# Two-layer graph network on one Trainium2 core: first gathers of the large aggregation issued in its own block, and two table stores moved to GpSimd's queue

## The reference

```python
# layer 0: 4 heads of 256, D_IN = 1024
xp = (x @ W).reshape(N, H, C)
e = leaky_relu(a_src[src] + a_dst[dst])           # edges and self loops
alpha = softmax of e over the edges of one dst
out = segment_sum(xp[src] * alpha, dst) + bias
x = layernorm(x + relu(out))
# layer 1: 1024 -> 256 -> attention with 4 heads of 64 -> 1024
h = rmsnorm(x) @ W_down
xl, xr = h @ Wl, h @ Wr
e = att . leaky_relu(xl[src] + xr[dst])
x = layernorm(x + segment_sum(softmax(e) * xl[src], dst) @ W_up)
```

## Time and profile before

| | us |
|---|---|
| median of 3 runs | 2424.14 (2420.76 to 2429.64) |
| profiled execution: its own time | 2423.4 |
| its span, first to last instruction | 2421.6 |
| projection block, with its boundary | 123 to 636 |
| large aggregation | 636 to 1209 |
| node block | 1209 to 1447 |
| edge scores of layer 1 | 1447 to 1991 |

### The profile page before, as it was taken

The page is one execution under the profiler, slowest core; times in us unless marked ns, Lnnn a source line. Parts: engine busy times, 40 slices in busy tenths (PEclk is TensorE's granted clock), DMA queues, the critical chain, the costliest instruction groups (busy, mean ns, idle before and its releaser), DMA issues. The chain is left out here.

```text
span 2421.6 us, 50236 instructions
## 1 busy us (share of the span) xinstructions
PE 1890.9 (78%) x10689; PEld 1240.5 (51%) x10690; DVE 1622.0 (67%) x4091; ACT 845.9 (35%) x2902; POOL 1377.3 (57%) x1421
## 2 busy tenths in 40 slices
PE   3988888887488888888848866877777773799797
PEld 2543334434266665666546654555555552667543
DVE  6345455448566666666668856656666569799987
ACT  1300000001477777777746633000000002455465
POOL 1077777771477777777600008777777762566500
PEclk9989999998799999999979988999999996899999
DMA  6433333220599999999899936888888873777457
GB/s 230 120 87 71 68 76 74 65 54 18 196 363 356 360 361 356 361 361 360 324 277 275 281 130 189 246 230 251 242 234 243 230 224 106 251 250 257 162 186 225
DMA packets 255893, 529.81 MB, mean 219 GB/s; under 512 B 52188, under 2 KB 148197, under 8 KB 255769
## 3 DMA queue, kind: packets, MB, share of 16 engines
q0 software_dynamic: 92672, 258.83, 33.2%
q1 hardware_dynamic: 125251, 225.64, 28.3%
q10 hardware_dynamic: 37878, 44.27, 6.7%
HBM read 439.07 MB, written 102.49 MB: 224 GB/s over the span
## 5 line engine op out<-in xcount | busy, mean ns | idle before, releaser
L155 POOL DMA_INDIRECT acc<-xl_table,csrc x392 | 400.6, 1022 | 354.6 <-POOLq L1299 235.4
L1195 ACT ACTIVATE wone<-onehot,w 128x64 f32<-128x64 f32 x1760 | 432.2, 333 | 166.1 <-DVE onehot L1239 162.1
L155 POOL DMA_INDIRECT ga<-a_src_table,csrc x316 | 315.8, 999 | 156.7 <-issue 143.8
L1212 PE MATMUL banks<-w_sb,wone 128*64 128x256 f32 x2368 | 315.6, 392 | 93.8 <-ACT wone L1195 45.2
L930 PE MATMUL banks<-w_sb,acc 128*128 128x512 f32 x800 | 381.5, 622 | 0.0
L155 POOL DMA_INDIRECT w_sb<-xp_table,isrc x296 | 293.9, 993 | 148.3 <-DMA xp_table<-xp_st 58.4
L1235 DVE TENSOR_TENSOR acc<-banks,acc 128x512 f32 x440 | 304.3, 692 | 0.3 <-issue 0.3
L1664 PE MATMUL banks<-xr_parts,onehot_t 128*128 x1320 | 188.1, 286 | 127.9 <-issue 102.6
L1796 PE MATMUL banks<-msg,onehot 128*128 128x265 f32 x880 | 216.5, 400 | 37.2 <-POOL msg L1766 17.4
L1692 DVE SCALAR_TENSOR_TENSOR prod<-banks,att_relu 128x1024 f32<-128x1024 f32 x110 | 134.7, 1224 | 163.9 <-ACT w L1629 157.5
L1664 PEld LDWEIGHTS banks<-xr_parts,onehot_t 128*128 128x128 bf16 x1320 | 127.2, 96 | 211.5 <-issue 172.2
(11 more groups left out here) (315 smaller groups left out, 2746.2 us busy)
## 6 DMA issues: line engine op xcount, KB each, us to landing
edge_rows<-acc SPq DMA_DIRECT2D x440, 130.0 KB
rows<-edge_rows SPq DMA_DIRECT2D x55, 1040.0 KB, 4.9
lt_bc<-local_dst ACTq DMA_DIRECT2D x110, 128.0 KB, 3.0
lt<-local_dst ACTq DMA_DIRECT2D x110, 128.0 KB, 4.3
xp_table<-xp_st SPq DMA_DIRECT2D x25, 512.0 KB, 2.9
w<-acc SPq DMA_DIRECT2D x100, 128.0 KB, 3.5
xpt<-xp_table SPq DMA_DIRECT2D x25, 512.0 KB, 4.9
x_table<-y SPq DMA_DIRECT2D x25, 512.0 KB, 7.0
```

What stands on the lines that cost most here:

```text
L155: return self.pool.indirect_dma_start(out, None, table, bass.IndirectOffsetOnAxis(ap=idx, axis=0), bounds_check=self.bound, oob_is_err=False)
L1195: last = nc.scalar.activation(wone[:, s, j, h, :], onehot[:, s, j, :], ACT.Copy, scale=w9[:, bass.ds(g * U + j, 1), h:h + 1].rearrange("p ...
L1212: nc.tensor.matmul(psum[WN * a:WN * (a + 1), j, k * C:(k + 1) * C], wone[:, s, j, h, :], slots[r][:, j, h * C:(h + 1) * C], start=True, st ...
```

## The change

It has two parts. In the first, POOL no longer issues gathers in the projection block: all 440 are issued in the aggregation block, behind the clearing of slots 22 to 24, which moves there too, and behind the wait for the stores. Slots 12 to 15 are cleared by ACT, as four activations that copy with scale 0, behind `take_weights`; slots 16 to 19 by DVE, two at a time between its `first_weights`. DVE waits for the stores of `xp_st` before it clears `rows_c`, and for POOL's clearing (`s_zero`) before its first addition. In the second part the stores of `x1` and `xl` are issued by POOL, with lags 3 and 6 in place of 4 and 7. A third edit only writes a bounded register value to a register of its own.

```diff
@@ projection block, POOL
-                    gather.wait(s_xp, NT)
-                    for i in range(2):
-                        gather.wait(s_xs[i], 16 * ((NT + 1 - i) // 2))
-                    for g in range(FIRST):
-                        for j in range(U):
-                            gather.rows_of(rows[:, g, j, :], xp_t, isrc[:, g * U + j:g * U + j + 1]).then_inc(s_r[g][j], 16)
-                    nc.gpsimd.memset(acc[:, NU:NT, :], 0.0)
@@ projection block, ACT, at its end
+                    for i in range(4):
+                        nc.scalar.activation(acc[:, KEPT + i, :], bc(pidx[:], [P, D]), ACT.Copy, scale=0.0)
@@ projection block, DVE, at its end
-                    for b in range(NB):
+                    first_weights(0)
+                    dve.wait_ge(scan["m"], NB)
+                    for b in range(1, NB):
                         first_weights(b)
-                    nc.vector.memset(acc[:, KEPT:KEPT + 4, :], 0.0)
+                        if b < NB - 1:
+                            nc.vector.memset(acc[:, KEPT + 2 + 2 * b:KEPT + 4 + 2 * b, :], 0.0)
                     evict_xp(24, 0, 12)
-                    nc.vector.memset(acc[:, KEPT + 4:KEPT + 8, :], 0.0)
@@ aggregation block, POOL
+                    nc.gpsimd.memset(acc[:, NU:NT, :], 0.0).then_inc(s_zero, 1)
                     gather = PoolGather(pool, N, bound)
-                    gather.wait(s_clr, 1)
-                    for i in range(FIRST * U, T):
+                    for i in range(2):
+                        gather.wait(s_xs[i], 16 * ((NT + 1 - i) // 2))
+                    for i in range(T):
                         g, j = i // U, i % U
+                        if i == 2 * U:
+                            gather.wait(s_clr, 1)
                         gather.wait(s_mm, i - 3 * U + 1)
@@ node block, POOL
+                    def store_x1(t, s, m):
+                        s2, m2, s3, m3 = slots(s, m)
+                        order.wait(S["x1"], t + 1)
+                        pool.dma_start(x1_t[bass.ds(t * P, P), :], y[:, s3, :]).then_inc(s_x1s[s3], 16)
...
+                    pipelined(pool, NT, [(3, store_x1), (6, store_xl)], AHEAD, 6)
@@ node block, SP
-                    pipelined(sp, NT, [(0, load_sums), (0, load_weights), (0, load), (4, store_x1), (7, store_xl)],
+                    pipelined(sp, NT, [(0, load_sums), (0, load_weights), (0, load)],
```

More of the change, by code:

```diff
@@ L759, in gnn_kernel @@
         scan = ScanSems(sem)
-        s_clr = sem("memory_cleared")
+        s_clr = sem("rows_cleared")
+        s_zero = sem("sums_cleared")
         s_r = [[sem(f"p2_r{i}_{j}") for j in range(U)] for i in range(3)]
         rows = w_sb[:].rearrange("p (g j) n -> p g j n", g=2)
-        FIRST = 2
         with ExitStack() as ph:
@@ L1001, in _ @@
                     last_group = dve.alloc_register("p1_last")
+                    group_of = dve.alloc_register("p1_last_bounded")
                     def onehots(g, i, s, m):
@@ L1226, in group @@
                             ds = tiles.load(g - 1)
+                        if isinstance(g, int) and g == 1:
+                            dve.wait_ge(s_zero, 1)
                         for j in range(U):
@@ L1242, in group @@
                                 if isinstance(g, int) and g == 0:
+                                    for i in range(2):
+                                        dve.wait_ge(s_xs[i], 16 * ((NT + 1 - i) // 2))
                                     nc.vector.memset(rows_c[:], 0.0).then_inc(s_clr, 1)
@@ L1304, in _, with store_xl @@
                     nc.gpsimd.memset(eps[:, 1:2], RMS_EPS).then_inc(S["clr"], 1)
+                    order = PoolGather(pool, N, bound)
+                    def store_x1(t, s, m):
+                        s2, m2, s3, m3 = slots(s, m)
+                        order.wait(S["x1"], t + 1)
+                        pool.dma_start(x1_t[bass.ds(t * P, P), :], y[:, s3, :]).then_inc(s_x1s[s3], 16)
+                    def store_xl(t, s, m):
+                        s2, m2, s3, m3 = slots(s, m)
+                        order.wait(S["sf"], t + 1)
+                        pool.dma_start(xl_t[bass.ds(t * P, P), :], xls[:, s2, 0:XLW]).then_inc(s_xls[s2], 16)
+                    pipelined(pool, NT, [(3, store_x1), (6, store_xl)], AHEAD, 6)
                 @block.sync
@@ L1594, in _ @@
                     last_group = sp.alloc_register("q1_slast")
+                    group_of = sp.alloc_register("q1_slast_bounded")
                     def store_rows(g, s, m):
@@ L1601, in store_rows @@
                         sp.reg_alu(last_group, chunks.regs[U - 1], 2, ALU.logical_shift_right)
[L1602 to L1603 removed]
+                        sp.reg_alu(group_of, last_group, 0, ALU.max)
+                        sp.wait_ge(s_fetched, sp.snap(group_of, min_val=0, max_val=NGC - 1) + 1)
                         wait(sp, s_xe[s], 64 * m)
@@ L1645, in _ @@
                     last_group = pe.alloc_register("q1_last")
+                    group_of = pe.alloc_register("q1_last_bounded")
                     def group(g, s2, m):
@@ L1653, in group @@
                         pe.reg_alu(last_group, chunks.regs[U - 1], 2, ALU.logical_shift_right)
-                        pe.reg_alu(last_group, last_group, 0, ALU.max)
-                        done = pe.snap(last_group, min_val=0, max_val=NGC - 1) + 1
+                        pe.reg_alu(group_of, last_group, 0, ALU.max)
+                        done = pe.snap(group_of, min_val=0, max_val=NGC - 1) + 1
                         pe.wait_ge(s_ot, g + 1)
```

12 lines of the change are left out of this document (2 added, 10 removed).

## The result

The changed kernel takes 2385.8 us (median of 4 runs, 2382.9 to 2391.4), the kernel before 2424.7 (4 runs): a ratio of 0.984, with its 95% interval [0.9815, 0.9867]. The forecast was 2396 us, within 2387 to 2410. The profiled execution took 2384.8 us, its span is 2383.1.

What follows compares the result with a forecast made beforehand. Bounds: when the aggregation's row of gathers, 1.298 us each, starts, and node-block tiles held by late stores. From the profiled execution, 2423.4 - 17.1 - 9.6 - 5.0 + 4.0 = 2395.7, taken as 2396 us; range 2387 to 2410.

Steps and rivals of the forecast that it cites:

- The first boundary: Projection to aggregation: barrier at 611.0 us with ACT last, first gather at about 614.3, 17.1 us gained.
- rival 2: First boundary: the 8.2 us are a fixed cost of POOL entering the block, not the gathers'; 2404 us, chance 0.05.
- the 8.2 us: First boundary, kernel before: POOL's DRAIN ended 8.2 us behind its last clearing, and all engines waited for POOL.
- The tiles: Node block: without the store waits, 20 tiles take 7.61 us each instead of 8.09, 9.6 us gained.
- The ceiling of 0.978: Node block: highest DMA share seen in a long stretch; 7.44 us of work per tile divided by it gave 7.61.
- rival 3: Node block: DMA has room, so tiles take DVE's 7.2 us; 2388 us, chance 0.10.
- That a second queue fills the gaps of the first: Node block: one queue was 91.6% busy and a second fills its gaps; given as reason for taking 9.6 us.
- Rival 1: Node block: the DMA engines are full already, tiles stay at 8.09 us; 2405 us, or 2410 with the hole; chance 0.17.
- The last two tiles: Node block's end: with stores in their own queue, about 7.3 us each instead of 19.6 together; 5.0 us gained.
- The end of the block: Node block: POOL's last store and a 5.2 us DRAIN make 6.5 us instead of 2.5, a loss of 4.0.
- Rival 4: Node block: POOL's stores land late, issue up to 3.3 us; 2408 to 2418 us, chance 0.10, of it 0.03 slower.

Runs made afterwards that it cites:

- early_clear: Changed kernel, but POOL clears slots 22 to 24 at the projection block's end again, behind the last product; 3018.1 us, 0.9873 of the kernel before.
- half_relu: Changed kernel, but DVE adds relu and input for only 512 of 1024 columns in the node block; 3008.5 us, 0.9847 of the kernel before.
- sp_first: Kernel before, but SP's list for each tile has both stores ahead of the copies and loads; 3025.1 us, 0.9934 of the kernel before.
- act_stores: Changed kernel, but ACT's queue issues the stores of x1 and xl instead of POOL's; 3010.5 us, 0.9870 of the kernel before.

## Why the prediction was right in direction and too small

- *The first boundary* (17.1, measured 16.5). Right: ACT last, first gather within 0.1 us of the forecast, then one row of gathers at 1.299 us (570.2 / 439). The four activations took 0.97 us each, not 1.14, and the weights before them came 1.4 us later, so ACT ended 0.5 us late; the 0.5 us that the forecast left between the clearing and the first gather were not needed. That the errors cancelled to 0.1 us is luck.
- *Why the barrier was late.* The forecast took POOL's DRAIN for waiting on the gathers. `early_clear` shows a tail of 7.6 us with no gather near it, so rival 2 was right that the 8.2 us were not the gathers' alone, but wrong to place them at POOL's entry: the tail stands behind POOL's last instruction in any block in which it has issued DMAs. Its price of 8.2 us did not come, because the change ends POOL's work 54 us before the barrier. The forecast gained its 17.1 us without the right reason for the tail, since by either reason it goes when POOL ends early.
- *The tiles* (9.6, measured 18.1): the step that failed. The prediction said that "the DMA engines have 8.09 x 0.92 = 7.44 us of work per tile" and divided it by 0.978 (the 8.09 are those of nine tiles; the twenty took 8.02). Neither figure was what it was taken for. The ceiling of 0.978 was none: the share is 0.99 in the changed kernel and 1.00 in `half_relu`. And the busy time was no fixed work: over the same 19 tiles it fell from 7.3 us a tile (7.94 x 0.92) to 7.0 (7.08 x 0.99) with the same bytes. A share of 0.99 or 1.00 stood for 304 GB/s (`sp_first`, `combine` 3 to 22), 317 (changed kernel) and 329 (`half_relu`); a packet's time holds waiting for others. The packets of 4096 bytes in SP's queue show it in the trace of before: alone on one engine (1409 to 1412 us) each took 159 ns; in the 19 tiles they took 159 ns in the median too, but 205 on average, and one in ten over 319. That the stores were late because of their place in SP's list was right, and `sp_first` shows it; what the tiles had left was DVE's 7.2 us in the loop and 6.89 ahead of it: rival 3, with 0.10. Of the 10.8 us by which the sum fell short, 8.5 are this term. Perfetto Trace Analysis of the Trainium skill (Identifying the Most-Contended Engine) says to judge DMA by the bandwidth moved "instead of occupancy", which the rows here bear out: the earlier trace rows show 280 GB/s, while the same shapes later ran at 329.
- *That a second queue fills the gaps of the first* was a wrong reason too: `sp_first` has nearly the same tiles in one queue. Rival 1, full DMA engines, falls with the 317 GB/s. On "Issuing engines are not separate DMA queues" of the page DMA: Bandwidth & Descriptors (Trainium skill) the trace agrees that the engine of issue hardly matters (POOL, ACT and SP all gave tiles of 7.2 us). That held, and still the tiles got shorter: the place in an issuer's list decided when a store started.
- *The last two tiles* (5.0, measured 3.6). The mechanism was right, one engine for the 53 rows; the stores no longer wait behind them, but the load itself is 1.7 to 2.2 us late for the last `combine`. The forecast had called it due in time.
- *The end of the block* (4.0, measured 2.8). Right: a DRAIN, 4.1 us behind the last store instead of 5.2, and 0.55 us for the store itself instead of 1.0.
- *Rival 4* did not come: POOL issued its 50 stores in 0.54 us each, none stretched toward the 3.27 us of the earlier trace rows, and the `x1` store landed in 6.1 us instead of 7.4 (medians, 1320 to 1380 us). By the GPSIMD Engine Reference's rule on shared SBUF interfaces (Trainium skill, Key points) these issues would have been stretched beside `combine`; the measurement shows none that was.

## What to carry to other kernels

Before moving a store to another queue, see where it stands in its issuer's list: here two stores moved to the front of the same list gave 16 of 19 us of the gain in the tiles. Do not take a DMA busy share for work, nor the highest share seen so far for a ceiling; take the busiest engine's work per tile as the bound, and test it by taking half an operation away. Let POOL end early in a block in which it has issued DMAs, and cut a ragged last tile so that its row count divides among the DMA engines.

## What was unexpected of the hardware

- A DRAIN of POOL ends 2.8 to 9.5 us behind its last instruction in every block where it issued DMAs, even when those had landed over 60 us before (7.6 us, `early_clear`), and within 0.13 us of it in the other blocks named above. What sets the size stays open.
- POOL's queue sends fewer packets: with the two stores there, the kernel has 2399 packets fewer for the same 529.81 MB (3200 fewer under 2 KB). The packets' sizes tell why: 3200 fewer of 1040 bytes in SP's queue and 800 more of 4160 in POOL's, so four rows went together. `act_stores`, without this, was no slower.
- The same program takes 2424 us on some chips and 3050 on others. The node block, whose transfers are loads and stores of whole tiles, takes the same time on both.
